# Query and key columns with the heads innermost, and three stacked loads in place of six

## What is computed

```python
q = norm(x) @ Wq + bq        # 2048 x 256, split into heads of 16 (L0, L1, L3) or 32 (L2) columns
k = ctx @ Wk + bk            # 1601 x 256, split in the same way
v = ctx @ Wv + bv
att = softmax(q_head @ k_head.T * scale)      # per head, 2048 x 1601
x = x + concat(att @ v_head) @ Wo + bo
```

## Time and profile before

| | us |
|---|---|
| median of 3 runs | 3858.27 |
| fastest, slowest of the 3 | 3856.71, 3861.03 |
| the profiled execution | 3857.22 |
| its span in the trace | 3855.5 |
| TensorE busy with matmuls | 3615.5 (94%) |
| VectorE busy | 2536.7 (66%) |
| ScalarE busy | 1931.5 (50%) |
| GpSimd busy | 645.9 (17%) |

### The profile page before, as it was taken

The page is one execution under the profiler, slowest core; times in us unless marked ns, Lnnn a source line. Parts: engine busy times, 40 slices in busy tenths (PEclk is TensorE's granted clock), DMA queues, the critical chain, the costliest instruction groups (busy, mean ns, idle before and its releaser), DMA issues. The chain is left out here.

```text
span 3855.5 us, 50411 instructions
## 1 busy us (share of the span) xinstructions
PE 3615.5 (94%) x17554; PEld 1563.8 (41%) x17555; DVE 2536.7 (66%) x5373; ACT 1931.5 (50%) x2358; POOL 645.9 (17%) x940
## 2 busy tenths in 40 slices
PE   5999999799999999987997899999799999998996
PEld 2333333365533333325665333333433333332564
DVE  5888888456678888844223655553478888884523
ACT  3677777521147777762332444444203777777111
POOL 3200001200041010014221301010313001001242
PEclk8999999899999999998999899999799999999998
DMA  6300000123000000025001400000140000001144
GB/s 129 54 19 16 17 18 6 50 75 77 24 30 15 18 14 19 9 65 202 31 30 50 114 20 16 18 18 5 58 94 31 18 18 15 18 10 49 53 121 133
DMA packets 132653, 171.33 MB, mean 44 GB/s; under 512 B 38379, under 2 KB 106589, under 8 KB 130257
## 3 DMA queue, kind: packets, MB, share of 16 engines
q1 hardware_dynamic: 119280, 142.27, 13.2%
q0 software_dynamic: 10144, 26.08, 2.7%
q10 hardware_dynamic: 3008, 0.15, 0.1%
HBM read 131.27 MB, written 40.84 MB: 45 GB/s over the span
## 5 line engine op out<-in xcount | busy, mean ns | idle before, releaser
L1524 DVE TENSOR_REDUCE mx<-ps 128x1 f32<-128x400 f32 (+1 forms) x3584 | 1818.4, 566 | 495.3 <-PE ps L2259 483.9
L1257 ACT ACTIVATE probs<-ps,zero_col 128x1024 f32<-128x1024 f32 (+1 forms) x1040 | 1111.1, 1111 | 585.0 <-PE ps L2295 584.6
L2259 PE MATMUL ps<-k_stack,q_stack 97*128 97x400 bf16 (+1 forms) x3584 | 1076.5, 339 | 50.1 <-DMA k_stack<-k_parts 27.8
L2295 PE MATMUL ps<-q_stack,k_stack 100*128 100x512 bf16 (+2 forms) x3328 | 1056.9, 381 | 6.4 <-ACT probs L1257 6.4
L2309 PE MATMUL ps<-probs,v 128*32 128x512 f32 (+2 forms) x5824 | 891.5, 607 | 0.2 <-ACT probs L1257 0.2
L2259 PEld LDWEIGHTS ps<-k_stack,q_stack 97*128 97x128 bf16 x3584 | 290.4, 97 | 1049.2 <-DVE mx L1524 624.8
L1257 ACT ACTIVATE probs<-ps,mask_col 128x1024 f32<-128x1024 f32 (+1 forms) x416 | 439.5, 1110 | 158.6 <-PE ps L2295 158.6
L2295 PEld LDWEIGHTS ps<-q_stack,k_stack 100*128 100x128 bf16 (+2 forms) x3328 | 323.3, 100 | 345.0 <-ACT probs L1257 65.8
L2309 PEld LDWEIGHTS ps<-probs,v 128*32 128x32 f32 (+2 forms) x5824 | 140.1, 111 | 264.3 <-issue 248.8
L1674 DVE SCALAR_TENSOR_TENSOR x_res<-ps,comb,x_res 128x256 f32<-128x256 f32 x336 | 148.1, 479 | 63.0 <-PE ps L2559 57.5
L1325 ACT ACTIVATE h_t_s<-ps 128x512 f32<-128x512 f32 x80 | 47.8, 597 | 254.3 <-PE ps L2550 254.3
(11 more groups left out here) (293 smaller groups left out, 2715.0 us busy)
## 6 DMA issues: line engine op xcount, KB each, us to landing
q_stack<-q_parts SPq DMA_DIRECT2D x384, 64.0 KB, 2.2
q_parts<-qk_part SPq DMA_DIRECT2D x32, 384.0 KB, 2.5
w_up<-in_up SPq DMA_DIRECT2D x17, 704.0 KB
w_up_s<-in_expert SPq DMA_DIRECT2D x40, 256.0 KB, 2.7
k_stack<-k_parts SPq DMA_DIRECT2D x48, 200.1 KB, 7.1
k_stack<-k_parts POOLq DMA_DIRECT2D x48, 200.1 KB, 4.1
k_parts<-qk_part SPq DMA_DIRECT2D x24, 384.0 KB, 3.1
w_all<-in_up SPq DMA_DIRECT2D x8, 1024.0 KB, 12.6
```

Source lines behind the costliest of these rows:

```text
L1257: act.activation(PR[pair[0] % 4][0:r, :, :], PS[0:r, 2 * b:2 * b + 2, :], ACT.Exp, bias=mask_col[0:r, k:k + 1] if L == 3 else zero_col[0:r ...
L1524: ins = dve.reduce_max(MX4[g % 2][:, u, c:c + 1], PS[:, bank, 0:CK[c]], AX.X)
L2259: last = mm(PS[:, bank, 0:CK[c]], QS[g][0:97, slot_of(j), qt * P:(qt + 1) * P], KS[0:97, (g * hpg + j) * nsub, CKO[c]:CKO[c] + CK[c]], sta ...
L2295: last = mm(PS[0:r, b + i, :], KS[0:rows, (g * hpg + jj) * nsub + sub, k * P:k * P + r], QS[g][0:rows, slot_of(jj) + sub, :], start=sub == ...
```

## The change

`q_parts` and `k_parts` get the layout `[2 halves, 3 parts, 128, tokens]`, and within the 128 columns of a half the order is "column of the head, then head": the heads are innermost. The columns of Wq, Wk, bq and bk are put in this order on the host (`heads_last`). The stores write the same bytes in the same number of rows. The six blocks of a stack are put in another order, keys 0 0 0 1 1 2 and queries 0 1 2 0 1 0, which gives the same six products. `KEY_LOADS` and `QUERY_LOADS` list the loads as (slot, first block, number of blocks, first part, step of the part). With step 1 a load brings consecutive parts, and its source is one run of equally spaced rows. With step 0 and more than one block it brings the same part into two or three blocks: its source gets a first axis of length n that repeats (`unsqueeze(0).to_broadcast([n] + ...)`).

- Keys in L0, L1 and L3: three loads, of three blocks (a repeat of part 0), two blocks (a repeat of part 1) and one block, in place of six. In L2: four loads, of one, one, one and three blocks (the last with step 1).
- Queries in L0, L1 and L3: three loads, of three, two and one blocks, step 1. In L2: five loads, the first of two blocks.
- GpSimd's loads in L1 and L3 are made at every second unit of the dense work instead of every unit. The waits count the new numbers.

```diff
-PRODUCTS = [(0, 0), (1, 0), (0, 1), (2, 0), (1, 1), (0, 2)]
+KEY_LOADS = {1: [(0, 0, 3, 0, 0), (0, 3, 2, 1, 0), (0, 5, 1, 2, 0)],
+             2: [(0, 0, 1, 0, 0), (0, 1, 1, 0, 0), (0, 2, 1, 1, 0), (1, 0, 3, 0, 1)]}
+QUERY_LOADS = {1: [(0, 0, 3, 0, 1), (0, 3, 2, 0, 1), (0, 5, 1, 0, 0)],
+               2: [(0, 0, 2, 0, 1), (0, 2, 1, 0, 0), (1, 0, 1, 2, 0), (1, 1, 1, 1, 0), (1, 2, 1, 0, 0)]}
...
-    q_parts = nc.dram_tensor("q_parts", [3, D, T], bf16, kind="Internal").ap()
-    k_parts = nc.dram_tensor("k_parts", [3, D, S], bf16, kind="Internal").ap()
+    q_parts = nc.dram_tensor("q_parts", [2, 3, P, T], bf16, kind="Internal").ap()
+    k_parts = nc.dram_tensor("k_parts", [2, 3, P, S], bf16, kind="Internal").ap()
...
-        def load_keys(eng, L, g, rows=(0, 6)):
+        def stacked(parts, L, g, load):
+
+            dh, hpg = ATT[L]["dh"], ATT[L]["hpg"]
+            _, _, n, part, step = load
+            rows = parts[g // 2].rearrange("r (d h) s -> (r d) h s", h=P // dh)
+            heads = slice(g % 2 * hpg, (g % 2 + 1) * hpg)
+            if step == 0:
+                src = rows[part * dh:(part + 1) * dh, heads, :]
+                return src.unsqueeze(0).to_broadcast([n] + list(src.shape)) if n > 1 else src
+            return rows[part * dh:(part + n) * dh, heads, :]
+
+        def load_keys(eng, L, g, loads=(0, 4)):
...
-            for i in range(*rows):
-                part, _ = PRODUCTS[i]
-                src = k_parts[part].rearrange("(h d) s -> d h s", d=dh)[:, g * hpg:(g + 1) * hpg, :]
-                r, sub = (i, 0) if nsub == 1 else (i % 3, i // 3)
-                eng.dma_start(KS[r * dh:(r + 1) * dh, 4 * g + sub:4 * g + 4:nsub, :], src).then_inc(done, 16)
+            for load in KEY_LOADS[nsub][slice(*loads)]:
+                sub, r, n = load[0:3]
+                dst = KS[r * dh:(r + n) * dh, 4 * g + sub:4 * g + 4:nsub, :]
+                eng.dma_start(dst, stacked(k_parts, L, g, load)).then_inc(done, 16)
...
-                dst = k_parts[:, m * P:(m + 1) * P, c * Q:c * Q + n].rearrange("r p t -> p r t")
+                dst = k_parts[m, :, :, c * Q:c * Q + n].rearrange("r p t -> p r t")
...
-                if a["nsub"] == 1:
-                    for row, (_, part) in enumerate(PRODUCTS):
-                        src = q_parts[part].rearrange("(h d) t -> d h t", d=dh)[:, g * hpg:(g + 1) * hpg, cols]
-                        sp.dma_start(dst[row * dh:(row + 1) * dh, :, :], src).then_inc(s_ql[buf], 16)
...
+                for load in QUERY_LOADS[a["nsub"]]:
+                    sub, r, n = load[0:3]
+                    rows = dst[r * dh:(r + n) * dh, sub::a["nsub"], :]
+                    sp.dma_start(rows, stacked(q_parts, L, g, load)[:, :, cols]).then_inc(s_ql[buf], 16)
...
-                    for i in range(6 * NG):
-                        pool.wait_ge(s_y, results.at() + per_unit * (begin + i))
-                        load_keys(pool, L + 1, i // 6, (i % 6, i % 6 + 1))
+                    for i in range(3 * NG):
+                        pool.wait_ge(s_y, results.at() + per_unit * (begin + 2 * i))
+                        load_keys(pool, L + 1, i // 3, (i % 3, i % 3 + 1))
...
+    def heads_last(m, dh):
+
+        m = m.reshape(*m.shape[:-1], 2, P // dh, dh)
+        return np.swapaxes(m, -1, -2).reshape(*m.shape[:-3], D)
```

More of the change, by code:

```diff
@@ L531, in store_query_parts @@
                 sp.wait_ge(s_qp, qp.at())
-                dst = q_parts[:, m * P:(m + 1) * P, c * Q:(c + 1) * Q].rearrange("r p t -> p r t")
+                dst = q_parts[m, :, :, c * Q:(c + 1) * Q].rearrange("r p t -> p r t")
                 sp.dma_start(dst, QP[buf][:]).then_inc(s_qd[buf], 16)
@@ L626, in first_queries @@
                 if L == 2:
-                    load_keys(sp, 2, 0, (2, 6))
+                    load_keys(sp, 2, 0, (2, 4))
                 wait_landed(qd)
@@ L2208, in begin_maxima @@
                 for g in range(NG):
-                    ks_queues[L % 2][g].step(6 * 16)
+                    ks_queues[L % 2][g].step(len(KEY_LOADS[ATT[L]["nsub"]]) * 16)
                 for q in range(3):
-                    ql[q].step(7 * 16)
+                    ql[q].step((1 + len(QUERY_LOADS[ATT[L]["nsub"]])) * 16)
             def attention_jobs(L):
@@ L2399, in iteration @@
                         if not (last and g > 0):
-                            ql[(g + 3) % 4].step(7 * 16)
+                            ql[(g + 3) % 4].step((1 + len(QUERY_LOADS[nsub])) * 16)
                         mr.step(16)
@@ L2786 @@
         a[f"wo{L}"] = pairs_of_groups(a[f"wo{L}"], ATT[L]["hpg"])
+        for n in ("wq", "wk", "bq", "bk"):
+            if f"{n}{L}" in a:
+                a[f"{n}{L}"] = heads_last(a[f"{n}{L}"], ATT[L]["dh"])
     a["gw0"], a["gw1"] = w["L0_ffn_gate_weight"].T, w["L1_ffn_router_w"].T
```

## The result

The changed kernel takes 3909.65 us (median of 4 runs, 3901.90 to 3912.48) against 3859.65 us for the kernel before on the same chip: a ratio of 1.0125 [1.0107, 1.0144], slower by about 50 us. The direction and the few engines were as forecast, the size was not: 3869 us was the forecast, with 3877 us as the upper end. The profiled execution took 3908.09 us.

A forecast was written before the change was run, and what follows sets the result against it. TensorE, busy 94% of the span, was taken as the bound, so DMA edits matter only where it waits. Sum: 3857.2 + 11.3 (L0 transfer and staging) + 3 (clock) - 2.5 (L3) = 3869.0 us; range 3847 to 3877.

The forecast's parts named there:

- The choice between the ends of the transfer: L0's key loads: either spread over 16 engines or on three and two; took the few engines, chance 0.65.
- Rival A: Key loads spread over 16 engines: L0 -5.1 us, L3 about -3.5, together -10, 3847 us, faster; chance 0.22.
- B: Rival: the transfer rate stays, only issues are saved, 1.35 us in L0 and 1.9 in L3: 3854 us; chance 0.12.
- C: Rival: few engines, L0's group 0 late by 4.9 us, but staging slack, clock stays: 3857 to 3862 us; chance 0.12.
- The size of the transfer, +4.9 us: L0's group 0 keys: busiest engine moves 423 KB at 26.2 GB/s, 16.1 us; keys there at 59.3, not 54.45.
- The staging chain, +11.3 us: L0: store of query unit (0, 1) lands at 77.3, delaying evacuations; TensorE waits 7.7 us at its first turn; sum so far +11.3.
- The clock, +3 us: L0: the 7.7 us gap at 78.5 brings back TensorE's low clock, +3 us (0 to 4.5).
- L0's groups 2 and 3, 0: Their keys load beside the scores, there after 18 us, needed 23 us on: 0, at a margin of 5 us.
- L1, 0: Group 0's last key load goes some 40 us before the first maxima, slowest load takes 7.8 us: 0.
- L2, 0: Key and query loads have no repeated first axis; its start waits for VectorE, not loads: 0 (-1 to +1).
- L3, -2.5 us: L3's start: three fewer query issues, -1.9 us; query store up to 3.5 us sooner or 5 later; range -5.4 to +3.
- The saved issues: Three fewer query loads save 1.35 us ahead of L0's keys and 1.9 in L3; elsewhere SyncE's slack, 0.

The follow-up runs named there:

- experiment 4: Experiment 2 with key parts padded to 136 rows in DRAM, so merged loads have a first axis of three or two without repeats: 3901.94 us, 1.0109.
- experiment 7: Changed kernel with the three-block key load in L0, L1 and L3 split into a repeated pair and a single: 3892.85 us, ratio 1.0098.
- experiment 8: Experiment 2 with L2's two part 0 loads made one-head loads into two blocks 32 rows apart, repeated first axis of two: 3861.80 us, 1.0005.
- experiment 6: Changed kernel with GpSimd's key loads of groups 2 and 3 in L1 and L3 held back by 14 units: 3881.91 us, ratio 1.0061.
- Experiment 5: Changed kernel with repeated key loads in L0 only; L1 and L3 get six one-block loads from GpSimd: 3885.92 us, ratio 1.0077.
- experiment 1: Changed kernel with keys of L0, L1 and L3 in six one-block loads again, new layout and three query loads kept: 3853.33 us, ratio 0.9990.
- experiment 2: Changed kernel with blocks reordered so no load repeats: three key loads and four query loads of consecutive parts; 3851.16 us, ratio 0.9982.
- experiment 3: Changed kernel with the key loads' repeat as second axis, queries of L0, L1 and L3 in six strided loads: 3864.91 us, ratio 1.0016.

## Why the prediction was right in direction and wrong in size

Two kinds of step failed. The rate of each of three engines under the triple load was taken as 26.2 GB/s, and it was half of that for two of them. And three terms were put at 0, 0 and -2.5 us (L0's groups 2 and 3, L1, L3) that measured +8.7, +11.9 and +8.6: they cost the most.

**The choice between the ends of the transfer** was right: a share of 0.19, 3 of 16 engines, where I had written near 0.2. The Trainium skill, DMA: Bandwidth & Descriptors, section Rules for kernel authors, puts it on the slowest axis longer than 1, with the leading repeat as its example; the trace agrees, and experiment 4 shows (1.0109) that an axis of three needs no repeat for it. Rival A falls by the share, B by the 67.67, C by the waits.

**The size of the transfer, +4.9 us, was +13.2.** The step that failed is "at 26.2 GB/s": I took the engine's full rate for each of three engines, 79 GB/s. They moved 54 in 48 to 58 and 76 only in 58 to 62. In the packet records of the trace one of the three needs 0.48 us for each row of 12,808 bytes, 26 GB/s, and the other two 0.8 to 1.0 us, in step with each other, until they are through their rows of the triple load at 57.7. One of these two goes on with 16 rows of the pair load and its row of the last block. Its 16 rows of the triple load take from 42.30 to 57.7, 15.4 us where I had 7.8; the 17 rows behind take 9.3 us, most of them at 0.48, to 67.08, and TensorE starts at 67.67. What halves the two is open: experiment 7 says that it goes with the triple load, and experiment 8 that a distance of 32 rows alone isn't enough.

**The staging chain, +11.3 us, was +19.5** at the first turn (94.45 against 74.92): the right chain with the wrong rate in it once. The store landed +19.4 us (85.43 against 65.99), and of the 8.1 us beyond my 77.3 all stand already in group 0's keys, 67.67 for 59.3. Group 1's keys took what I had given them: in the packet records the three engines reach its triple load one after the other, and their rows take 0.48 us. TensorE stands at L2163 for 5.69 us and at L2332 for 3.08 us where I had one wait of 7.7 us.

**The clock, +3 us,** is the difference between the chain and the first scores: 140.08 against 117.55 is +22.5, 3.0 more than the first turn. The low stretch is there, PEclk 0.50 in 88 to 98. This step was right, as far as a difference can show it.

**L0's groups 2 and 3, 0, were +8.7 us.** I looked only at whether the keys would be there in time. They were. But TensorE's next need on that queue is the row maxima: their reload follows their store 10.4 us later now (168.69, 179.05), while rows of the key loads are still moving until 177.2, and TensorE waits 3.84 us for it. Before, it was 1.4 us:

```profile
146.80 0.31 SPq L593 DMA_DIRECT2D m_parts<-m_part  x1
148.24 0.26 SPq L598 DMA_DIRECT2D q_stack<-m_parts  x1
```

An idle TensorE loses its clock, which I had applied once and not here; the granted clock behind the wait:

```profile
182.00:184.00 2.00, 2.00 (x7) 0.69 (x5) 1.35 (x4) 1.11 (x1) 0.00 (x0) 0.50 0.03 8
...
188.00:190.00 2.00, 2.00 (x9) 0.65 (x11) 1.33 (x3) 1.59 (x2) 0.00 (x0) 0.50 0.46 118
190.00:192.00 2.00, 2.00 (x12) 0.38 (x5) 0.65 (x2) 0.60 (x1) 0.00 (x0) 0.73 0.02 4
```

Ten us at the level of 1.2 GHz cost about half of them, an estimate that fits what is left: 31.2 - 22.5 - 3.8 = 4.9 us.

**L1, 0, was +11.9 us.** I had worked out that the keys themselves come in time, and they do. The step left out what else uses the engines: the parts of the first query tile on the busy ones, whose last counts come up to 13 us after the others (experiment 6). The wait is 10.1 us of the 11.9.

**L2, 0,** was right: between the marks nothing is lost there.

**L3, -2.5 us, was +8.6.** I had named the mechanism, "it waits for its share on the busy ones", gave it +5 and then took the other side of the range. The store took 12.5 us (2874.29 to 2886.80) where 7.0 us were measured before. The first query tile behind it makes the rest: from the first load's issue to TensorE's start it is 9.3 us (2886.80 to 2896.08) where it was 6.1 (2838.30 to 2844.40), although three issues are saved. Experiment 5 replaces the key loads beside it and experiment 6 moves them away, and the wait is 8.2 and 8.0 us, as before the change. The row in my hands was that very store, already slow beside the key loads; it should have weighed more than the saved 1.9 us.

**The saved issues** are worth little: experiment 1 keeps those of the queries, experiment 2 most of both, without the few engines, and they gain 4.5 and 6.7 us, of which the earlier start of the maxima is 2.2 us.

Of the 40.6 us between forecast and time, L0's start makes 22.5 - 14.3 = 8.2 us, groups 2 and 3 make 8.7, L1 makes 11.9 and L3 makes 8.6 + 2.5 = 11.1, together 39.9. Four fifths lie in the last three, terms that I had set at zero or below: for the first two I asked only when the keys arrive, and for L3 I named the delay and bet against it.

One slip of the prediction has no weight: its parts add to 0.30 for "same" and 0.16 for "faster", where it says 0.29 and 0.17.

What stays open: why two of three engines run at half their rate; whether experiment 6, with L0 as changed, is really quicker than experiment 5 (4 us by the medians of four runs each, with intervals that overlap); and the 11 us of experiment 3 over experiment 1.

## What to carry to other kernels

When loads are merged, look at the first axis of the result, not at the count of loads: an axis of two or three puts everything on two or three engines, whether it repeats a source or not. Often the order of the blocks can be chosen so that the merged load reads consecutive rows (experiment 2, 0.9982), which keeps the fewer issues without the price. And a transfer on few engines must be costed twice: once for who waits for it, and once for each DMA beside it that is spread over all engines, on another queue too.

## What the runs showed of the hardware that I had not expected

- Three engines that began one load of three blocks together moved 54 GB/s, no more than two did (48 to 53), and one alone 26. After that load, the rate of the same three was 76.
- A store that needs all engines took 15.8 us in L1 beside such loads, 2.8 without them, and 12.5 us in L3, where it had been 7.0. The key loads were on GpSimd's queue, the store on SyncE's: the other queue did not help.
- Most of the counts of a DMA came long before the last: with two engines busy 14 of 16 by 2130.03 and the last at 2141.11 (experiment 8), with three busy 13 of 16 by 922.85 and the last at 935.20.
- A wait of 3.84 us was enough to bring TensorE to 1.2 GHz for ten us, so that it cost more than twice its length.
- At the same DMA share near 1 the rate differed: in 44 to 54 us 142 GB/s before and 158 in experiment 1, both with key loads of one block, and 180 in experiment 2 with loads of three and two. Query loads fall into the same stretch.
